# Moving the last chunk's shared expert behind the routed tiles, and another order of steps in the last attention group

## What is computed

```python
x = x + attention(layernorm(x))            # ternary weights, causal, rms_norm on q, k and on the output
xf = layernorm(x)
scores = sigmoid(xf @ w_router); top_vals, top_idx = top_k(scores, 2)      # normalised to sum 1
for e in range(8):
    he = silu(xf @ w1[e]) * (xf @ w3[e]);  out = out + combine[:, e:e+1] * (he @ w2[e])
shared = silu(xf @ ws1) * (xf @ ws3) @ ws2                                  # inner width 352
x = x + out + shared
```

## Time and profile before

| | us |
|---|---|
| median of 3 timed runs | 596.61 (595.45 to 596.68) |
| the profiled execution, own time | 590.83 |
| its span | 589.0 |
| PE busy in the span | 490.4 (83%) |
| last group of attention, last values matmul | ends near 400.7 |
| first tile's up matmul | starts at 479.21 |
| last scatter of a tile | starts at 566.68 |
| last addition of the end | starts at 583.13 |

### The profile page before, as it was taken

How to read it: one execution, slowest core, us unless ns; L and a number is a source line. 1 busy time by engine, 2 the same in 40 slices (tenths; PEclk the granted TensorE clock), 3 DMA queues, 4 the chain that set the end, 5 groups by cost and what they waited for, 6 DMA issues and landing times.

```text
span 589.0 us, 10118 instructions
## 1 busy us (share of the span) xinstructions
PE 490.4 (83%) x3328; PEld 276.6 (47%) x3328; DVE 340.9 (58%) x972; ACT 364.2 (62%) x567; POOL 166.8 (28%) x221
## 2 busy tenths in 40 slices
PE   1586889997999999999989888939697979999930
PEld 1583323233333333333334333417585869998920
DVE  6975566843581235812246766364967757666626
ACT  4253778883899878998777867535452335555520
POOL 4501101011101021010242227125455834444430
PEclk9887989897999999999999999779799899999975
DMA  8999999000000000000132003122011333444349
GB/s 230 299 304 306 279 7 2 2 1 1 1 1 1 1 2 1 1 0 1 37 99 86 26 1 114 45 85 73 15 60 48 94 101 101 125 124 120 110 139 344
DMA packets 66390, 49.84 MB, mean 85 GB/s; under 512 B 24552, under 2 KB 64072, under 8 KB 66344
## 3 DMA queue, kind: packets, MB, share of 16 engines
q1 hardware_dynamic: 62936, 39.89, 30.1%
q0 software_dynamic: 3408, 9.34, 4.4%
HBM read 19.88 MB, written 29.34 MB: 84 GB/s over the span
## 4 chain that ended last, share of the span: by engine, by line
PE 58%; DVE 16%; issue 11%; ACT 4%; POOL 4%; DMA 4%; SPq 1%; ACTq 0%; POOLq 0%; DVEq 0%
PE ps L1479 18%; PE ps L1459 12%; PE ps L1662 6%; PE ps L1443 5%; PE ps L1680 3%; ACT prob L696 3%; PE ps L1608 2%; PE ps L1488 2%; PE ps L1409 2%; DVE qk L973 2%; PE ps L1684 2%; POOL rows_by_expert L580 1%; PE ps L1671 1%; DMA yfin<-pair_out 1%; PE ps L1653 1%
## 5 line engine op out<-in xcount | busy, mean ns | idle before, releaser
L696 ACT ACTIVATE prob<-ps 128x1024 f32<-128x1024 f32 (+3 forms) x320 | 262.3, 916 | 85.3 <-PE ps L1459 84.3
L1479 PE MATMUL ps<-prob,v_sb 128*32 128x512 f32 (+3 forms) x1280 | 157.9, 567 | 12.2 <-POOL prob L539 8.5
L1459 PE MATMUL ps<-qk 50*128 50x512 f32 (+3 forms) x640 | 120.4, 441 | 8.9 <-ACT prob L696 5.6
L539 POOL TENSOR_SCALAR_AFFINE_SELECT prob<-prob 128x512 f32<-128x512 f32 x64 | 41.2, 645 | 253.4 <-ACT prob L696 253.2
L1459 PEld LDWEIGHTS ps<-qk 50*128 50x128 f32 x640 | 53.7, 193 | 92.8 <-ACT prob L696 69.1
L973 DVE CAST qk<-ps 128x512 fp32r<-128x512 f32 (+1 forms) x48 | 33.1, 691 | 68.7 <-PE ps L1443 68.7
L1479 PEld LDWEIGHTS ps<-prob,v_sb 128*32 128x32 f32 x1280 | 25.8, 110 | 57.6 <-issue 28.7
L641 POOL DMA_INDIRECT pair_out<-yo,xg x39 | 37.4, 959 | 54.3 <-DVE yo L1345 54.0
L1443 PE MATMUL ps<-ident,stack 128*128 128x128 f32 x192 | 33.0, 297 | 10.5 <-DVE qk L973 8.5
L1443 PEld LDWEIGHTS ps<-ident,stack 128*128 128x128 f32 x192 | 21.2, 146 | 42.6 <-issue 41.7
L1608 PE MATMUL ps<-x2T,ws_hi 128*128 128x512 f32 (+1 forms) x96 | 32.4, 420 | 5.1 <-DVE hid L1214 5.1
(11 more groups left out here) (205 smaller groups left out, 802.7 us busy)
## 6 DMA issues: line engine op xcount, KB each, us to landing
rows_by_expert<-pads SPq DMA_DIRECT2D x9, 1935.0 KB, 20.6
xg<-rows_by_expert SPq DMA_DIRECT2D x39, 129.0 KB, 2.2
yfin<-pair_out SPq DMA_DIRECT2D x8, 512.0 KB, 7.0
stage<-in_w SPq DMA_DIRECT2D x8, 352.0 KB
x_sb<-in_x SPq DMA_DIRECT2D x4, 512.0 KB, 6.2
res<-in_x SPq DMA_DIRECT2D x4, 512.0 KB, 4.0
out<-y_sb SPq DMA_DIRECT2D x4, 512.0 KB, 5.2
stage<-in_w SPq DMA_DIRECT2D x8, 176.0 KB
```

The lines of the kernel that those rows point to most:

```text
L539: nc.gpsimd.affine_select(out=t, in_=t, compare_op=ALU.is_ge, fill=0.0, base=0, pattern=[[0, HPG], [1, P]], channel_multiplier=-1).then_in ...
L696: nc.scalar.activation(prob[:, u % NPB, 2 * hf:2 * hf + 2, c0:CH], ps[:, b:b + 2, c0:CH], ACT.Exp, scale=SCALE).then_inc(exp_done, 1)
L1459: ins = M(ps[:, 2 * (n % NSB) + h, c0:CH], qk[rows, par, PAIRS, kt * P:(kt + 1) * P], qk[rows, par, hf, j * CH + c0:(j + 1) * CH], start=T ...
L1479: ins = M(ps[VW * h:VW * (h + 1), O_BANK, c0:CH], v_sb[:, kt, :], prob[:, u % NPB, h, c0:CH], start=(kt == 0), stop=(u == LAST_OF[j]), ski ...
```

## The change

It moves work and changes no arithmetic.

- In the last group most steps come one unit earlier, steps 5 and 6 of chunk 2 move from the shared stage into it, and in the shared stage the steps come in another order (`AFTER`). DVE's list is reordered to match.
- Pieces 7 and 8 are no longer split inside attention. POOL splits pieces up to 10 (before: 14), DVE the eight w2 pieces 11 to 18 (before: 15 to 18), ACT writes the high parts of 7 to 18, one in each shared step from n = 0 on.
- The last chunk's three shared steps, n = 9 to 11, run behind the last tiles. Their low parts on POOL stand behind the tiles' scatters; the low parts of n = 5 to 8 move to DVE.
- The first tile's up waits for pieces up to 10, its down for all 19.

```diff
-SHARED_PIECES, EARLY_PIECES, POOL_PIECES = KD + 1, 9, 15
+SHARED_PIECES, EARLY_PIECES, POOL_PIECES, UP_PIECES = KD + 1, 7, 11, KD + 1 + 4 * KD
-    24: [("out", 0, 2)], 26: [("step", 4, 1)], 27: [("step", 5, 1)], 28: [("step", 0, 2)], 29: [("step", 1, 2)],
+    24: [("out", 0, 2)], 25: [("step", 4, 1)], 26: [("step", 5, 1)], 27: [("step", 0, 2)], 28: [("step", 1, 2)],
-LATE_PIECE_AT = {1: 9, 2: 10, 3: 11, 4: 12, 5: 13, 6: 14, 8: 15, 9: 16, 11: 17, 12: 18}
+LATE_PIECE_AT = {n: n + 9 for n in range(10)}
-LOW_PIECES = {3: range(0, 3), 11: range(3, 5), 23: range(5, EARLY_PIECES)}
+FLAT_FIRST = (NC - 1) * SH
+LOW_ON_DVE = range(5, FLAT_FIRST)
...
 # POOL, last group
+                if u == TPC * NC * (NC - 1) // 2 + TPC * (NC - 1):
+                    send_rows(1, 0)
                 if on_diagonal(u):
                     mask(NKV - 1, u)
...
 # DVE
             row_stats(0, LN)
+            scale_x2(0)
             output(g, 1)
-            scale_x2(0)
...
             choose(0)
+            row_stats(1, LN)
             place(0)
+            scale_x2(1)
+            high_piece(5)
             copy_output(g, 2)
-            row_stats(1, LN)
             take_output(g, 2)
-            scale_x2(1)
...
+            row_stats(2, LN)
             choose(1)
             place(1)
-            row_stats(2, LN)
...
             hidden(5)
+            place(3)
+            low_piece(12)
+            hidden_low(5)
             hidden(6)
+            list_tiles()
+            low_piece(13)
+            hidden_low(6)
+            hidden(7)
+            low_piece(14)
+            hidden_low(7)
             take_shared(1)
             hidden(8)
             low_piece(15)
+            hidden_low(8)
             low_piece(16)
             low_piece(17)
             low_piece(18)
...
+            for c in range(NC - 1):
+                finish(c)
+                if c == 0:
+                    hidden(FLAT - 1)
+            take_shared(NC - 1)
+            finish(NC - 1)
...
 # PE, tiles
                 if i >= 2:
                     tile_down(i - 2, expert[i - 2])
+                if i >= TILES:
+                    up(FLAT_FIRST + i - TILES)
+            for n in range(FLAT_FIRST, FLAT):
+                down(n)
+                if n + 2 < FLAT:
+                    up(n + 2)
```

180 lines of the change are left out of this document (99 added, 81 removed).

## The result

The changed kernel takes 615.62 us, the median of four runs (614.22 to 622.76), beside 596.03 us for the kernel before (594.33 to 596.68) in the same series. The ratio is 1.036, with a 95% interval from 1.029 to 1.043. The medians are 19.6 us apart, where the prediction said 13 and had a range up to 619. The ratio is one of means and counts a fifth run of the changed kernel (618.48); it comes to 21.6 us.

What follows compares the result with a forecast made beforehand. Bounds: PE's 8.49 us wait before unit 36, two chains before the first tile, and the additions after the last scatter. +8.7 (first tile), +1 (clock), +3.2 (end) made +12.9, forecast 609.5 us; range 599 to 619.

Steps and rivals of the forecast that it cites:

- part 4: Weight pieces before the first tile: rounds of load, ACT high part and DVE low part put first up at 487.9, +8.7.
- rival B: New PE stalls before the tiles bring more stretches at the lower clock: +20, 616.6 us; chance 0.18.
- Part 1: DVE's later output copies in the last attention group: unit 12 near 324.2, unit 24 at 358.2, step 4 of chunk 1 +3.
- the steps keep their time: Last group, chunk 0: step 4 still comes near 327.5, only attention falls one unit, 1.7 us, behind.
- Part 2: Masks before unit 36: scatters of chunk 1 replace the pieces, unit 36 starts 2.7 later, stall some 5 for 8.49; group +3.6.
- Part 3: Chunk 3's routing, with choose(2) moved behind it: row numbers at 449.3 against 457.8, 8.5 us earlier.
- the ring: Staging buffers before the first tile: each piece's load waits for the low part two pieces before; 7.0 us a round.
- Rival A: Before the first tile, the pieces don't bind and routing sets it, 21.4 after row numbers: 591.3 us; chance 0.13.
- a first tile released by the transfer of its rows: Sign at the first tile's start, named as showing the prediction wrong; no size given.
- Part 5: After the tiles: up(9) makes the last scatter +2.4, and DVE with take_shared(3) sets the last addition, +3.2.

Runs made afterwards that it cites:

- e10: Kernel before with only three staging buffers of 512 columns for pieces 11 to 18; ratio to the kernel before 0.997 (0.993 to 1.002).
- e3: Changed kernel with three staging buffers of 512 columns in place of two of 768 for pieces 11 to 18; ratio to the kernel before 1.013.
- e2: Changed kernel with the first four scatters of chunk 1 moved behind the masks of units 36 to 39 on POOL; ratio to the kernel before 1.026.
- e12: Kernel before with only DVE's two output copies (chunks 1 and 2) moved later, PE's order unchanged; ratio to the kernel before 1.011.
- e4: Kernel before with only POOL's low parts of pieces 7 and 8 moved behind the masks of units 36 to 39; ratio to the kernel before 0.994.
- e11: Kernel before with only the last attention group's order on PE and DVE changed as in the change; ratio to the kernel before 1.016.
- e8: Changed kernel with the group's old order, scatters behind masks, three buffers, and up(9) behind the last tile's down; 596.84 us, ratio to the kernel before 0.997.
- e6: Changed kernel with up(9), silu(9) and hidden(9) put behind the last tile's down; ratio to the kernel before 1.034.
- e9: e8 plus pieces 11 to 13 and hidden_low(5) on POOL, chunk 2's router step later, hidden(11) before the additions; 593.92 us against 598.85, ratio 0.989.

## Why the prediction was right, and where its sum was short

The direction, the places of the waits and the mechanism of part 4 were right, and the time lies inside the range. But the sum was 12.9 against 19.6 (21.6 by the ratio), so a third or more is missing, and both lie above the +7 to +18 that the prediction gave its own sum. The range held the result because it also took in rival B, and because an error in part 4 offset some of those in parts 1 to 3; that much was luck. Stage by stage, with the row numbers taken at their end (457.8 before, 468.9 in the changed kernel):

| stage | forecast | the two profiles |
|---|---|---|
| group, to `take_output(3)` | +3.6 | +17.6 |
| from there to the row numbers of chunk 3 | -12.1 | -5.5 |
| from there to the first tile | +17.2 | +14.0 |
| tiles | +3.4 | +4.1 |
| end | +0.8 | +2.9 |

The two profiles lie 12 us further apart than the medians, most of it in the group: between e10 and e3 it grew by 7.8 only.

**Part 1, the term that was mis-sized.** The delay of each copy was read well, and both stalls are released by `o_sb`: unit 12's 3.45 for "3 to 4", unit 24's 3.91 (5.07 in e2 and e3), at or below the low end of "5 to 7". The step that failed is the sentence after it, that "the steps keep their time". They don't. From the copy of chunk 0 to PE's `sel_b` row of chunk 0 51.1 to 53.8 us pass in the seven traces with the changed steps or copies (53.7 in the changed kernel), and 47.7 to 50.4 in the six with the old order. DVE's `choose(0)` thus comes 2.8 us later in the mean, and up to 6 from trace to trace. The work in front of the second copy comes on top: forecast as 6.0, it is 6.2 (from DVE's `sel_b` of chunk 0 to the copy 8.82 us, where it was 2.64). Step 4 of chunk 1, put at +3, starts at 368.25 in the changed kernel and at 365.26 in e3, against 359.66: +8.6 and +5.6.

**Part 2, the absorption that did not come.** The prediction let the stall of unit 36 swallow all but 2.7 us of unit 24's 6.4. It swallowed nothing of that: unit 24 was 11.2 late, unit 36 14.1. The stall is shorter (3.04 for 8.49) only because PE lost more still between the two units and came to it 19.6 us late. What POOL waits for there is DVE's routing of chunk 1 (the scatters' 25.77 for `slots`), and DVE was late by the whole amount; e12 shows the stall unchanged behind a late group. On the way the delay grew. These are DVE's rows of `rms_scale(2)` and PE's router row in e3, to be held against the same work in the kernel before, where L1093 takes 0.16 us and the router's sixteen matmuls 1.95:

```profile
373.52 0.52 DVE L1098 CAST w_hi<-stage 128x704 fp32r<-128x704 f32 x1
374.12 1.70 POOL L565 TENSOR_TENSOR w_lo<-stage,w_hi 128x704 fp32r<-128x704 f32 x1 [5.29 <-DVE w_hi L1098]
374.15 1.69 DVE L1122 TENSOR_TENSOR sm<-sm,mv 128x4 f32<-128x4 f32 x1
379.20 3.58 PE L1579 MATMUL ps<-wr,x2T 128*128 128x16 f32 x16 [3.17 <-DVE yT_lo L1138]
```

The high part of piece 6, moved in front of `rms_scale(2)`, was costed at its own 0.5 us. It also starts POOL's low part, during which one small instruction of DVE takes 1.69 instead of 0.16; PE waits 3.17 for what follows (1.22 before), and runs the router at 1.2 GHz (granted clock 0.50 there), 1.6 us longer. A moved step's price is also what it releases on another engine. Between e3 and the two samples of the old order the group lost 116.3 - 108.5 = 7.8 (e10) or 116.3 - 104.6 = 11.7 (e4, without the stall), e11 and e12 give 9.5 and 6.6 in time, and the prediction gave 3.6. That is 3 to 6 us of the 7 to 9 that the sum lacks; the rest is in part 3 and the end, less what part 4 had too much. The four scatters ahead of the masks, given as 5 us of stall, had 3.04, and in e2 their removal took 4.7 off the group.

**Part 3.** The time from `take_output(3)` to the end of `scale_x2(3)` was forecast as 23.1: it is 23.0 (442.44 + 1.38 - 420.80). From there to the row numbers 18.4 were forecast and 24.9 came (the forecast's own terms add up to 0.2 more than it says). PE had the router's step of chunk 3 ready at 459.3, 38.5 behind `take_output(3)` and not 33. PE had waited 4.54 us for DVE's low parts before `sel_b` of chunk 2, and then ran the next `down` and half of the next `up` at the lower clock. The delay by POOL was there, 1.5 us for the 1 forecast (`sel_b` 1.72, its like 0.18).

**Part 4.** Right in mechanism, the ring, and nearly in size. From row numbers to first tile 38.6 us were forecast, 35.4 came (35.6 from the start of the row numbers); the rounds of pieces 13 to 15 took 10.3, 6.4 and 7.5 us for 12.1, 7.0 and 8.2. Without the ring's wait it is 25.1 (e3). Rival A, that the pieces don't bind, is excluded by that, and its own number can be read: in e3 and e8 25 us and not the 21.4 that it assumed. In e3 PE turns the first tile's rows (486.19) right behind its last `down`, and these `down`s had waited 3.51 us for `take_shared(1)`, which stands between pieces in DVE's list.

One sign that the prediction named for being wrong did appear: "a first tile released by the transfer of its rows". PE waited 3.21 us for `xg`. It doesn't speak against the ring, since that transfer was asked for behind the load of piece 18, and with three buffers the wait is gone; but the prediction had only DVE's list as the way from the pieces to the tile and did not see SP's.

**The tiles and the end.** Forecast +1 for the clock of the first tiles and +2.4 for `up(9)`: measured 4.1, of which e6 gives 2.6 to `up(9)`, and e3, whose first tile starts at full clock, 1.7 to the start. The end was put at 0.8 behind the last scatter and took 2.9. Two parts were missed: the first addition starts 9.3 us behind the last scatter, where it is 7.8 in the kernel before, in e6 and in e8; and the two additions in a row take 5.83 where each took 2.48. Why the loads of the results serve DVE 1.5 us later is open. SP asks for the first of them equally soon, 2.6 us behind the last scatter (598.38, before 569.22), and where `up(9)` comes behind the last down the delay is gone (7.77 in e6). Part 5's verdict stands: DVE sets the end.

**Rival B, the clock,** was given 0.18 and 616.6, closer than the forecast's 609.5. Rows bear it out: in the two stages before the tiles the granted clock is 0.79 where it was 0.90 and 0.91, that is, by an estimate from these means and the two levels, 51 + 35 us at 1.2 GHz against 21 + 14. Over 23 runs of the kernel before in e9's series the mean clock lies between 0.902 and 0.926 and the time between 593.01 and 602.96; a straight line through them falls by 3.2 us for each 0.01. The four timed runs of the changed kernel have 0.889 to 0.905, a mean of 0.897, against 0.915 in those 23: by that line 0.018, an estimate of 6 us of the 20. The line is loose (correlation -0.71). By it the two profiles, at 0.889 and 0.92, would differ by 10 us through the clock, of the 12 by which they lie further apart than the medians. The Trainium skill's page "TensorE: Matmul & The Clock Gate", section "HAM oscillation", says that a matmul stage with idle gaps keeps falling back to the lower clock; the 0.79 in a group with stalls of 3 to 4 us agrees. But no run held the stalls and changed the clock alone, so the 6 us are a correlation, and whether the clock is more here than a consequence of the stalls stays open. e8 has more lowered time than the kernel before (58 against 34 us between 300 and 504) and is still no slower.

## What to carry to other kernels

When a step is moved, follow the thing that it was hiding behind: if the later wait is for the same engine that is now late, it will absorb nothing, however long it is. Count with a moved step what it releases on other engines, and with a ring of staging buffers the distance at which a load waits for its buffer: two buffers and two engines in turn made a round of 6 to 10 us that three smaller buffers in the same memory took away. A load that waits for its buffer also holds every load behind it in the same list, here the rows of the first tile. An idle time seen in a profile is worth what the next wait leaves of it: 8.49 us of PE were worth some 3.5, and the same three buffers were worth 14 us in one kernel and 1.6 in the other.
